# A Transformer block on one core: three transpositions move behind the second scores of their slot, and one rounding Identity moves behind the next exponential

## What is computed

```python
h = layernorm(x) * (1 + ca) + sa
q, k, v = heads(h @ Wq + bq), heads(h @ Wk + bk), heads(h @ Wv + bv)
scores = q @ k.T * 0.25 + position_bias * 8
x = x + ga * (softmax(scores) @ v @ Wo + bo)
h = layernorm(x) * (1 + cb) + sb
gate, y = fp4(h) @ fp4(w_gate).T, fp4(h) @ fp4(w_up).T
x = x + gb * (fp4(silu(gate) * y) @ fp4(w_down).T)
# fp4: q = GRID[searchsorted(MID, |v| / scale)] * sign(v) * scale, scale = max|block of 16| / 6
```

## Time and profile before

| | us |
|---|---|
| median of three runs | 3291.3 |
| lowest and highest run | 3290.97, 3291.54 |
| the profiled execution, its own time | 3290.7 |
| its span, from first to last instruction | 3288.8 |

### The profile page before, as it was taken

How to read it: one execution, slowest core, us unless ns; L and a number is a source line. 1 busy time by engine, 2 the same in 40 slices (tenths; PEclk the granted TensorE clock), 3 DMA queues, 4 the chain that set the end, 5 groups by cost and what they waited for, 6 DMA issues and landing times.

```text
span 3288.8 us, 67878 instructions
## 1 busy us (share of the span) xinstructions
PE 3150.3 (96%) x22404; PEld 1877.6 (57%) x22404; DVE 2822.5 (86%) x9960; ACT 2137.1 (65%) x3389; POOL 1720.8 (52%) x2104
## 2 busy tenths in 40 slices
PE   4899999999999999999999999999999999999985
PEld 1345565656656565655566555565665556656555
DVE  6678888888988888888888998888889888888865
ACT  2566676666666766666666666766666666666652
POOL 3415555555555555555555555555555555555455
PEclk7899999999999999999999999999999999999997
DMA  8344433334443324444233444332344423244000
GB/s 206 65 78 81 83 77 57 63 69 83 84 85 66 60 59 78 86 83 83 55 64 64 83 86 83 72 60 61 71 84 83 86 59 63 63 79 80 21 23 13
DMA packets 200187, 238.39 MB, mean 72 GB/s; under 512 B 23600, under 2 KB 178640, under 8 KB 199808
## 3 DMA queue, kind: packets, MB, share of 16 engines
q1 hardware_dynamic: 199840, 234.06, 36.9%
HBM read 164.57 MB, written 67.31 MB: 71 GB/s over the span
## 4 chain that ended last, share of the span: by engine, by line
PE 73%; issue 8%; DVE 7%; ACT 7%; POOL 4%; DMA 1%; DVEq 0%; SPq 0%; ACTq 0%; POOLq 0%
PE ps_x L676 21%; PE ps_o L665 11%; PE rings L630 11%; PE rings L647 11%; PE ps_x L704 6%; PE rings L633 4%; ACT probs L819 3%; PE ps_x L711 3%; POOL hidden L1356 2%; PE ps_x L722 1%; DVE scale L1107 1%; ACT tanh L928 1%; ACT magic L847 1%; DVE row_max L1072 1%; DVE hidden L1177 1%
## 5 line engine op out<-in xcount | busy, mean ns | idle before, releaser
L1072 DVE CUSTOM_DVE_ANT_0 rings<-rings,band_z 128x512 f32<-128x512 f32 x2048 | 1415.9, 696 | 98.2 <-issue 95.2
L819 ACT ACTIVATE probs<-rings 128x1024 f32<-128x1024 f32 x1024 | 1048.0, 1023 | 435.9 <-PE rings L633 434.8
L647 PE MATMUL rings<-k_rows,q_rows 120*128 120x512 bf16 x2048 | 789.4, 386 | 26.3 <-DVE row_max L1072 24.4
L630 PE MATMUL rings<-q_rows,k_rows 121*128 121x512 bf16 x2048 | 702.7, 383 | 30.5 <-ACT probs L819 28.0
L633 PEld LDWEIGHTS rings<-rev,band_t 128*128 128x128 f16 x5632 | 409.6, 98 | 289.4 <-issue 0.8
L665 PE MATMUL ps_o<-probs,values 128*32 128x512 f32 x4096 | 545.6, 605 | 0.0
L633 PE MATMUL rings<-rev,band_t 128*128 128x64 f16 x5632 | 500.7, 192 | 0.0
L647 PEld LDWEIGHTS rings<-k_rows,q_rows 120*128 120x128 bf16 x2048 | 197.2, 96 | 493.6 <-DVE row_max L1072 380.7
L1356 POOL TENSOR_TENSOR hidden<-hidden,inv 128x704 f32<-128x704 f32 x128 | 178.4, 1394 | 446.2 <-DVE inv L1111 446.2
L676 PE MATMUL ps_x<-w_gu_h,xq_h 128*128 128x512 f32 (+1 forms) x768 | 356.8, 465 | 1.1 <-DVE xq_l L1117 1.1
L1171 DVE SCALAR_TENSOR_TENSOR tanh<-tanh,ps_x 128x256 f32<-128x256 f32 (+1 forms) x384 | 152.7, 398 | 165.4 <-ACT tanh L928 163.2
(11 more groups left out here) (180 smaller groups left out, 6557.2 us busy)
## 6 DMA issues: line engine op xcount, KB each, us to landing
parts_dram<-parts SPq DMA_DIRECT2D x128, 384.0 KB, 2.6
q_rows<-parts_dram SPq DMA_DIRECT2D x384, 128.0 KB, 5.5
k_rows<-parts_dram SPq DMA_DIRECT2D x384, 128.0 KB, 8.0
mod_rows<-mod_rows_dram SPq DMA_DIRECT2D x32, 640.0 KB, 10.1
x_in<-in_x SPq DMA_DIRECT2D x32, 512.0 KB, 5.3
x_mid<-in_x SPq DMA_DIRECT2D x128, 128.0 KB, 2.0
out<-x_mid SPq DMA_DIRECT2D x128, 128.0 KB, 2.5
k_rows<-band_dram SPq DMA_DIRECT2D x2, 1024.0 KB, 9.5
```

Source lines behind the costliest of these rows:

```text
L630: mm(ps_s[:, bank, :], kr[0:ROW_MAX + 1, h, k0:k0 + P], qr[0:ROW_MAX + 1, h, :], start=True, stop=False)
L647: mm(ps_m[:, bank, :], q_rows[par][0:ROW_MAX, h, j * P:(j + 1) * P], k_rows[par][0:ROW_MAX, h, :], start=True, stop=True).then_inc(mscores ...
L819: A(prob_pair(s, j), ps_s, ACT.Exp).then_inc(exp_done, 1)
L1072: v.tensor_tensor_reduce(ps, ps, band_z[:, bias:bias + S], 1.0, LOWEST, ALU.add, ALU.max, row_max[:, par, 4 * h + j:4 * h + j + 1]).then_i ...
```

## The change

`m1`, `xT1` and `m0` move from position 1 to position 2 of their slots 2, 6 and 10. The table is now built with `batch` ahead of `group`, so at (2, 2), (6, 2) and (10, 2) they come before `hT0`, and the order of the jobs among each other, and with it the banks, is unchanged. The Identity L849 leaves position (3, 3): it is issued at (0, 0) of the next group, behind the exponential there, with the same wait for its Square. No instruction is added or dropped.

```diff
-    batch = {(0, 2): "v0", (2, 1): "m1", (3, 0): "v1", (4, 2): "v2", (5, 1): "xT0", (6, 1): "xT1", (7, 0): "p0",
-             (8, 2): "p1", (10, 1): "m0", (11, 0): "p2", (12, 2): "p3"}
+    batch = {(0, 2): "v0", (2, 2): "m1", (3, 0): "v1", (4, 2): "v2", (5, 1): "xT0", (6, 2): "xT1", (7, 0): "p0",
+             (8, 2): "p1", (10, 2): "m0", (11, 0): "p2", (12, 2): "p3"}
     return [(s, j, jobs[at]) for s in range(16) for j in range(4)
-            for jobs, at in ((group, (s % 4, j)), (batch, (s, j))) if at in jobs]
+            for jobs, at in ((batch, (s, j)), (group, (s % 4, j))) if at in jobs]
...
                             A(magic3[:], hidden[:, g % 2, :], ACT.Square, scale=ROOT).then_inc(f3_act.sem, 1)
-                            after(act, f3_act, u, "sq")
+                        if (r, j) == (0, 0) and it.has_tile(s, 2):
+                            after(act, f3_act, it.tile(s, 2), "sq")
                             A(magic3[:], magic3[:], ACT.Identity, bias=floor[:]).then_inc(f3_act.sem, 1)
```

## The result

The changed kernel takes 3267.1 us (median of 6 runs, 3262.75 to 3268.46), the one before 3290.9 (6 runs, 3289.6 to 3291.54). The ratio is 0.9926 [0.9914, 0.9938], so 0.74% faster. The forecast was 3270.0, range 3258 to 3284. The profiled execution after took 3262.75 us with a span of 3260.9. Of the six runs after, the two with a mean granted clock of 0.982 took 3262.75 and 3264.58 us, the three at 0.981 between 3267.07 and 3267.89, and the one at 0.980 took 3268.46. In the traces TensorE is at its lower level at both ends of the execution only (the first 140 us have a mean clock of 0.73 in both), so the runs differ there, and I read the mechanism in iterations of the middle, where the clock is 1.00.

A forecast was written before the change was run, and what follows sets the result against it. TensorE's own order sets the pace, with 28.0 us of waits for exponentials; 0.48 + 0.20 + 0.02 = 0.70 us per iteration, 30 times, is 21 us off the 3291.3 us median: 3270 us, range 3258 to 3284.

The forecast's parts named there:

- Slot 6: Moving four xT1 transpositions behind the second scores removes TensorE's wait for the exponential before slot 7: gain 0.48 us per iteration.
- rival C: The wait moves to projection p0, which needs xT1's later copies; slot 6 gives nothing, 3285 us; chance 8%.
- Slots 4, 8 and 12: The Identity there hid nothing; moving it delays ctx_h, but the maxima in slot 4 keeps 0.15 us of room: 0.
- Slot 10: One transposition moved saves 0.11 us, but slot 11's first maxima has only 0.02 us of room: gain 0.02 us.
- the lower end (0.11): Slots 2 and 3: at least 0.11 us survives, the room of slot 3's first maxima; up to 0.30 if VectorE follows.
- Rival D: VectorE's addition L1142 in slot 5 misses its turn behind GpSimd: slower by 0.30 us per iteration, 3300 us; chance 7%.
- the term for slots 0 to 3: Identity's move in slot 0 plus slot 2's transposition, after waits for VectorE's maxima signals: 0.20 us per iteration together.
- the two give-backs of slots 0 and 1: The fourth maxima of each slot would wait for VectorE, 0.09 and 0.18 us, cutting the Identity's 0.37 to 0.10.
- comes only 0.05 us earlier than before: Slot 0: with the Identity ahead of ctx_h, VectorE's signal gains only 0.05 us, so the fourth maxima waits 0.09.
- The 0.15 us by which VectorE was to be late in slot 1: GpSimd gets the constant 0.86 us later; idle 0.56 absorbs part, leaving 0 to 0.30 us, taken as 0.15.
- Rival A: Nothing is given back because VectorE follows TensorE everywhere: 1.07 us per iteration, 3259 us; chance 12%.
- the 60 to 90 new waits of L647: Sign expected in the profile: maxima L647 waiting about 0.1 us each for L1072 at (0, 3), (1, 3), (3, 0), (11, 0).

The follow-up runs named there:

- run 3: Kernel before the change with only the four transpositions of slot 6 (xT1) moved to position 2: 3278.5 us, ratio 0.9961.
- run 12: Changed kernel with ScalarE's two copies of xT1 in slot 6 put behind its copies of hT0: 3284.1 us, ratio 0.9981.
- run 2: Kernel before with only the Identity moved behind the next exponential, in all four groups, transposition jobs left in place: 3280.1 us, ratio 0.9965.
- run 5: Kernel before with the Identity moved behind the exponential only in slots 4, 8 and 12, not slot 0: 3290.5 us, ratio 1.0002.
- Run 9: Changed kernel with VectorE's scales of the FFN input behind the third reduction in slots 2, 6 and 10, unchanged in slot 14: 3263.2 us, ratio 0.9919.
- run 4: Kernel before with the Identity moved behind the exponential only from slot 15 to slot 0 of the next iteration: 3279.7 us, ratio 0.9965.
- run 10: Changed kernel with VectorE's scales behind the third reduction in slots 2, 6, 10, 14 and ScalarE's FFN-input Square behind the next slot's first exponential: 3256.3 us, ratio 0.9899.
- run 11: Changed kernel with only ScalarE's Square of the FFN input moved behind the first exponential of slots 3, 7, 11 and 15: 3258.3 us, ratio 0.9904.

## Why the prediction was right, and where its steps were off

**Right.** The bound, TensorE's own order with a few exponentials in its way, and the method, reading the loss from starts and not from idle time.

- Slot 6: forecast 0.48 us, measured 0.45 (run 3). The copies ended 0.18 us before the first matmul of `p0`, forecast 0.17 (0.11 with the signal). But the program waits for the copies ahead of that matmul's weight load, which the margin of 0.11 left out: the load waits for them, and the second matmul is 0.03 us late for it. In run 12, where the copies come 0.67 us later, weight loads and matmuls move with them, and in run 2, where the jobs stay, they stand as before. So rival C's mechanism was at work, at 0.03 us.
- Slots 4, 8 and 12: forecast 0, measured 0 (run 5), with 0.15 us of room in slot 4 as forecast.
- Slot 10: forecast 0.02, measured 0.01. The gain of 0.11 at (10, 0) came back as 0.10 at (11, 0). Run 9 shows that VectorE's signal took it. Slots 2 and 3 behaved nearly as the lower end (0.11) said: 0.12 won at (2, 0), 0.02 given back at (3, 0), 0.01 at (2, 1), so 0.09.
- Rival D did not happen: the addition L1143 never exceeded 1.35 us. In slot 5 it now starts 0.34 us before the end of GpSimd's instruction (1376.80 against 1375.42 + 1.72), where it was 0.98 before (1388.37 against 1389.35), so it waits less and lasts 0.61 us, not 1.27. That is nearer to a missed turn, too: D's mechanism stood 0.34 us away.

**Off: the term for slots 0 to 3,** 0.20 us forecast, 0.46 measured: 0.37 in slots 0 and 1 (runs 2 and 4), 0.09 in slots 2 and 3. The whole error is the two give-backs of slots 0 and 1, which I sized at 0.09 and 0.18 and which are both zero. An iteration thus took 95.93 us, not 96.15, and the sum would have been 0.91 x 30 = 27 us, or 3264. That is a little past the 0.9 us at which the forecast's own range ends; that the median still came within 3 us of 3270 is in part luck of the ends. Two steps failed:

1. That `ctx_h` "comes only 0.05 us earlier than before". Behind its first scores VectorE's signal for the fourth maxima came at 1350.58 - 1346.34 = 4.24 us; my 1362.56 - 1358.23 was 4.33. The missing 0.09 us is in ScalarE's queue. Before, the Identity started 1359.34 - 1358.52 - 0.79 = 0.03 us behind the end of the Square whose result it needs. After, the exponential starts 0.09 us before the end of that Square (1347.33 against 1347.42) and the Identity 0.11 before the end of the exponential (1348.23 against 1348.34). Here an instruction that waits for the one directly ahead on ScalarE starts 0.12 us later than one that need not. The rows of before had both: the 0.03 gap in slot 0, and the overlap, for which I took 0.04 us between Square and exponential (1359.27 against 1358.52 + 0.79), where it was 0.09. The rest of the 0.09 us is 0.01 to 0.03 us each at the Identity and at `ctx_h`. With it the maxima just fits.
2. The 0.15 us by which VectorE was to be late in slot 1. It is late, but by 0.49 us and not by up to 0.86, behind the longer addition L1191, and the idle 0.56 us ahead of the product take all of that. Besides, I held VectorE's place fixed in time while I moved TensorE. The tanh product waits for the tanh, and that for TensorE's products of the same slots, which come 0.37 us earlier: the tanh (L928, now L929) starts 7.67 us behind the first scores of slot 0, where it started 8.04 behind them. Behind the first scores of slot 0 the product L1171 stood at 1366.75 - 1358.23 = 8.52 us before, and L1172 stands at 1354.67 - 1346.34 = 8.33 after. It came earlier, not later, and it is now VectorE's own reduction that it stands behind. The signal came 7.15 us behind the second scores before (1368.34 - 1361.19) and 7.27 after (1356.21 - 1348.94), which is 0.12 more, within the room of 0.25. With the tanh where it was, by my estimate from these rows, the maxima would have waited 0.37 - 0.25 = 0.12 us.

Rival A gave back nothing anywhere, 1.07 us. The truth lies between it and the forecast: slots 0 and 1 as in A, slot 11 as in the forecast. Of the 27 us that 30 iterations give, the medians show 23.8 and the spans of the profiled executions 27.9. The difference lies at the ends of the execution, not in the iterations. The list of waits did not show the 60 to 90 new waits of L647: it has 33 for 35 before. In starts, the maxima of (0, 3), (3, 0) and (11, 0) do stand 0.06 us behind their signals, as forecast, at a cost of 0, 0.02 and 0.10 us; that of (1, 3) does not.

## What to carry to other kernels

When an engine is moved earlier, follow each engine that works from its results and move it too, until a row shows what holds it. To hold the other engine still makes give-backs that are not there. Then look at the queue orders, not only at the durations: a ready instruction behind a waiting one (the exponential behind the Identity in slot 0, the copy behind the Square at the end, `p0` behind the wrong copy) was worth 0.37 to 1.1 us each time, but only where TensorE waited for it; the same move in slots 4, 8 and 12 gave nothing. A wait ahead of a matmul holds its weight load too, which starts earlier than the matmul, so a margin is to be read there. The stretch at the end, where nothing covers a wait, is worth a look of its own. Where two chains are both at the bound, to shorten one pays nothing: in slot 15 the exponential came earlier in runs 10 and 11, and VectorE's reductions held the slot at the same length.

## What the runs showed of the hardware

- On ScalarE the Identity, which waits for the result of the Square directly ahead, started 0.03 us behind that Square's end, all 128 times. The instructions of slot 0 that need not wait started 0.09 to 0.11 before the end of the one ahead. The difference is 0.12 us. With the Identity 0.09 us later the fourth maxima of slot 0, which just fits, would have waited, by that estimate.
- The least distance from VectorE's signal to TensorE's matmul was 0.06 us, in every place where the maxima was late (slots 0, 3, 11 and 15). From the end of ScalarE's copies to the weight load that waited for them it was 0.11 us, after the change and in run 12.
- VectorE's addition L1142, with two SBUF inputs, ends 0.28 us behind the end of GpSimd's instruction whenever it starts inside one (126 of 128 times before, 127 as L1143 after; 0.278 to 0.288) and 0.19 to 1.07 us of that one are left. Alone it takes 0.43. One case: 1376.80 + 0.61 against 1375.42 + 1.72. That it waits for the end fits the rule of the Trainium skill, page "SBUF — State Buffer", section "Who interferes with whom", that the one that starts first keeps the shared port: by it L1143's 0.61 us hold a wait of some 0.18 beyond its shortest 0.43. The 0.34 us that were left of GpSimd's instruction are more than this wait; no row shows why some 0.15 us of the addition need not wait. The same rule accounts for L1191's 1.20 us in slot 0: it starts at 1351.39, inside GpSimd's L1330 (1350.78 to 1352.31), and ends 0.28 us behind it.
